# Group 0 of a decoder layer's attention: the softmax weights' low part ahead of the next maxima, the queries' low parts behind them

## The reference, cut to what matters

```python
q = (hidden_states @ Wq.T).reshape(b, s, H, D).transpose(0, 2, 1, 3)
scores = jnp.einsum('bhqd,bhkd->bhqk', q, k) * scale
scores = jnp.where(causal, scores, jnp.asarray(-1000000000.0, scores.dtype))
attn = jax.nn.softmax(scores, axis=-1)
out = jnp.einsum('bhqk,bhkd->bhqd', attn, v)
out = out.transpose(0, 2, 1, 3).reshape(b, s, H * D)
return out @ Wo.T
```

## Time and profile before

| | us |
|---|---|
| median of 3 executions | 1101.77 (1101.17 to 1103.44) |
| the profiled execution | 1102.57 |
| its span | 1100.8 |
| TensorE busy | 1061.0 (96% of the span) |
| VectorE busy | 905.5 (82%) |
| ScalarE busy | 530.6 (48%) |
| GpSimd busy | 410.9 (37%) |

### The profile page before, as it was taken

How to read it: one execution, slowest core, us unless ns; L and a number is a source line. 1 busy time by engine, 2 the same in 40 slices (tenths; PEclk the granted TensorE clock), 3 DMA queues, 4 the chain that set the end, 5 groups by cost and what they waited for, 6 DMA issues and landing times.

```text
span 1100.8 us, 19648 instructions
## 1 busy us (share of the span) xinstructions
PE 1061.0 (96%) x6229; PEld 565.9 (51%) x6236; DVE 905.5 (82%) x1861; ACT 530.6 (48%) x1081; POOL 410.9 (37%) x423
## 2 busy tenths in 40 slices
PE   6999988999999999999999999999999998969998
PEld 5976544555555555555555555555555554434443
DVE  7979588888797878788888888787978798889973
ACT  5665466545444545454545455454445454233420
POOL 2339654545343435344342434353434243000000
PEclk9999999999999999999999999999999999999999
DMA  8036156564454455454534554544445388224442
GB/s 318 11 106 240 39 113 145 139 140 96 126 136 114 98 138 137 107 131 114 136 101 118 133 120 110 134 124 114 107 118 138 81 194 235 103 42 89 100 97 86
DMA packets 229601, 135.74 MB, mean 123 GB/s; under 512 B 200112, under 2 KB 202288, under 8 KB 228656
## 3 DMA queue, kind: packets, MB, share of 16 engines
q1 hardware_dynamic: 229552, 135.11, 48.3%
HBM read 68.23 MB, written 17.83 MB: 78 GB/s over the span
## 4 chain that ended last, share of the span: by engine, by line
PE 85%; DVE 8%; ACT 3%; issue 2%; POOL 1%; DMA 1%; POOLq 0%; DVEq 0%; ACTq 0%; SPq 0%
PE ps L1710 82%; PE ps L1963 2%; ACT prob L1042 1%; DVE wo_sb L1196 1%; DVE prob L1435 1%; DVE h_b L1196 1%; PE ps L2034 1%; DMA wq_sb<-wo_in 1%; DVE prob_t L1196 1%; PE ps L1724 0%; DVE stats L1257 0%; DVE wq_sb L1196 0%; DVE o_t L1196 0%; DMA prob_t<-prob_s 0%; POOL prob L767 0%
## 5 line engine op out<-in xcount | busy, mean ns | idle before, releaser
L767 POOL TENSOR_SCALAR prob<-prob,row_inv 128x128 f32<-128x128 f32 (+3 forms) x256 | 203.3, 813 | 438.7 <-DVE row_inv L1406 438.7
L1710 PE MATMUL ps<-wo_sb,o_t 128*128 128x512 f16 x1536 | 351.3, 379 | 3.6 <-DVE x_sb L1417 3.6
L1710 PE MATMUL ps<-h_b,wq_sb 128*128 128x512 f16 x1524 | 345.6, 382 | 1.3 <-DVE wq_sb L1196 1.3
L1042 ACT ACTIVATE prob<-prob,neg_max 128x128 f32<-128x128 f32 (+3 forms) x256 | 140.6, 550 | 222.4 <-DVE neg_max L1441 222.4
L1710 PEld LDWEIGHTS ps<-h_b,wq_sb 128*128 128x128 f16 x1524 | 148.5, 98 | 179.9 <-issue 4.3
L1710 PEld LDWEIGHTS ps<-wo_sb,o_t 128*128 128x128 f16 x1536 | 147.3, 98 | 171.7 <-DVE x_sb L1417 6.3
L1417 DVE SCALAR_TENSOR_TENSOR x_sb<-ps,x_sb 128x512 f32<-128x512 f32 x256 | 174.0, 685 | 54.7 <-PE ps L1710 53.8
L1710 PE MATMUL ps<-prob_t,v_sb 128*128 128x128 f16 (+2 forms) x960 | 116.7, 275 | 7.2 <-DMA prob_t<-prob_s 7.2
L1710 PE MATMUL ps<-k_t,q_t 128*128 128x512 f16 (+3 forms) x768 | 114.8, 299 | 0.6 <-DVE neg_max L1441 0.6
L1435 DVE CUSTOM_DVE_ANT_0 prob<-ps,mask 128x512 f32<-128x512 f32 (+3 forms) x256 | 110.2, 483 | 2.3 <-issue 1.6
L1710 PEld LDWEIGHTS ps<-prob_t,v_sb 128*128 128x128 f16 x960 | 83.5, 98 | 37.6 <-DMA prob_t<-prob_s 8.0
(11 more groups left out here) (147 smaller groups left out, 1132.6 us busy)
## 6 DMA issues: line engine op xcount, KB each, us to landing
wq_in<-in_wq SPq DMA_DIRECT2D x64, 256.0 KB, 3.6
wo_in<-in_wo SPq DMA_DIRECT2D x32, 512.0 KB, 3.9
side_in<-in_ctx SPq DMA_DIRECT2D x16, 512.0 KB, 4.2
kv_parts<-wo_sb SPq DMA_DIRECT2D x7, 1024.0 KB, 5.4
x_sb<-in_x SPq DMA_DIRECT2D x8, 512.0 KB, 9.3
ctx_quantised<-side_out SPq DMA_DIRECT2D x16, 256.0 KB, 2.9
h_b<-ctx_quantised SPq DMA_DIRECT2D x2, 2048.0 KB, 11.0
out<-x_sb SPq DMA_DIRECT2D x8, 512.0 KB, 2.9
```

The costliest lines, as they stand in the source:

```text
L767: ins = nc.gpsimd.tensor_scalar(at, at, row_inv[:, u % 2, q:q + 1], S_P, ALU.mult, ALU.mult)
L1042: ins = nc.scalar.activation(at, at, ACT.Exp, bias=neg_max[:, n % 2, q:q + 1], scale=SOFTMAX, accum_out=row_sum[:, n % 2, q:q + 1])
L1710: ins = nc.tensor.matmul(out_, lhs(i), rhs(j), start=start and n == 0, stop=stop and n == 3 * len(pairs) - 1)
```

## The change

In group 0, from u = 1 on, VectorE takes p_split(g, u-1) ahead of maxima(g, u) instead of behind them. The low parts of the queries of step u-1, which stood at the end of step u-1, now come right behind maxima(g, u). The low parts of step 7's queries stay at the end of step 7. In all other groups the order is as it was. No other engine's list changes.

```diff
--- before.py
+++ after.py
@@ -1456,8 +1456,14 @@
                 for u in range(UNITS):
                     queries = not (last and u >= PAIR_UNITS)
                     s = u % PAIR_UNITS
+                    if first and u > 0:
+
+                        p_split(g, u - 1)
                     maxima(g, u)
-                    if not (first and u == 0):
+                    if first and u > 0:
+                        for unit in STEP_UNITS[(u - 1) % PAIR_UNITS]:
+                            q_part(g, u - 1, unit)
+                    if not first:
                         p_split(g, u - 1)
                     step_add(g, u, 0)
                     inverses(g, u)
@@ -1491,7 +1497,7 @@
                             combine(g, u, n)
                     step_add(g, u, 2)
                     step_add(g, u, 3)
-                    if queries:
+                    if queries and (not first or u == UNITS - 1):
                         for unit in STEP_UNITS[s]:
                             q_part(g, u, unit)
                     if s == 3 and not last:
```

## The result

The changed kernel takes 1114.01 us, the median of four executions (1112.41 to 1114.38), the kernel before beside it 1102.41 (1101.17 to 1103.44). The ratio is 1.0098, with a 95% interval of 1.0085 to 1.0110: slower by about 11 us. The forecast was 1112.3 us, with 1104.5 to 1116.0 as range, and a chance of 0.87 for slower.

What follows compares the result with a forecast made beforehand. TensorE, busy 85% of a 1100.8 us span, was taken as the bound, group 0's delay reaching the end. Adding 10.5 gave 1111.3, with 1.77 around it 1113.1, less 0.8 to the median 1112.3 us; range 1104.5 to 1116.

Steps and rivals of the forecast that it cites:

- H: Time when ScalarE's high part of the previous step's weights is ready; VectorE now stands at the step's head until then.
- C: End of VectorE's work of the previous step; neg_max(u) was to end at max(C, H) + 1.49 + 1.93.
- the carried shift: Delay of neg_max passed from step to step in group 0: +3.5 us in step 1, +11.1 in step 7.
- S(7): TensorE's scores of step 7 in group 0, forecast to start at 208.0 us instead of 198.73.
- The wait that I had set the sum on: TensorE's wo chunks of step 6 wait for VectorE's wo_sb low part, forecast to end at 196.6 us, not 185.96.
- SyncE: A Wq load of step 2 comes some 2.5 us later, its reader 5.85 us later: cost taken as zero.
- The clock: TensorE's clock drops after waits in group 0: taken as 0, though by the skill's rule 1.4 us more.
- Contention on p_lo: VectorE's low part of the weights slowed by GpSimd: taken as 0, bounded at 0 to 1.4 us each.
- Faster: Rival, chance 0.08: the transposes' 7.2 us and the clock's 1.4 go, giving 1093 us; decided at H = C.
- Half: Rival, chance 0.15: VectorE's work fits under GpSimd and the weights' high part, 10.45 us a step; 1104 to 1108 us.
- (a): Group 0's q_t low parts go behind the next maxima, under a 2.75 us wait; step 2's two took 3.07 us.
- (b): The previous step's low part of the weights goes ahead of the maxima, so VectorE stands until H in group 0.

Runs made afterwards that it cites:

- experiment 7: The changed kernel with a second PSUM bank for outputs(1) and outputs(3) of group 0: ratio 1.0083 to the kernel before, group 0 90.74 us.
- step 4 alone: The kernel before with VectorE's low part of the weights ahead of the maxima in step 4 of group 0 only: ratio 0.9998.
- experiment 6: The changed kernel, ScalarE taking the weights' high part before its q_t high parts, three of four group 0 normalising instructions left out: 1.0041; without leaving them out 1.0085.
- its control: The kernel before with the same ScalarE reordering and three of four normalising instructions left out in group 0: ratio 1.0010, group 0 81.1 us.
- experiment 2: The kernel before with only the q_t low parts moved behind the next maxima and the weights' low part in group 0: ratio 0.9961, 1099.95 against 1103.80 us.
- step 1 alone: The kernel before with VectorE's low part of the weights ahead of the maxima in step 1 of group 0 only: ratio 1.0024.
- the short normalising: Three of four GpSimd normalising instructions left out in group 0: ratio 0.9990 in the kernel before, 1.0085 in the changed kernel.

## Why the prediction was right

**The bound.** TensorE has no wait from 220 to 900 us in the changed kernel, so group 0's loss reached the end at full size. Right.

**The shifts, step by step.** The changed kernel's group 0 began 1.03 us late, which is taken off here. neg_max(1) to neg_max(7) end, by these rows, at 142.9, 153.3, 165.4, 178.8, 189.6, 201.6 and 214.0:

```profile
143.75 0.17 DVE L1441 TENSOR_SCALAR neg_max<-row_max 128x4 f32<-128x4 f32 x1
...
154.18 0.17 DVE L1441 TENSOR_SCALAR neg_max<-row_max 128x4 f32<-128x4 f32 x1
...
166.29 0.17 DVE L1441 TENSOR_SCALAR neg_max<-row_max 128x4 f32<-128x4 f32 x1
...
179.62 0.17 DVE L1441 TENSOR_SCALAR neg_max<-row_max 128x4 f32<-128x4 f32 x1
...
190.49 0.17 DVE L1441 TENSOR_SCALAR neg_max<-row_max 128x4 f32<-128x4 f32 x1
...
202.45 0.17 DVE L1441 TENSOR_SCALAR neg_max<-row_max 128x4 f32<-128x4 f32 x1
...
214.85 0.17 DVE L1441 TENSOR_SCALAR neg_max<-row_max 128x4 f32<-128x4 f32 x1
```

Forecast were 142.95, 153.45, 165.65, 179.55, 190.45, 202.5 and 214.7: each within 1 us. The largest new miss is step 4: I had kept the 2.38 us of the Wq block's low part, and it took 1.93, beside a GpSimd sum into ctx_sum that took 2.12 instead of 2.57. So H against C and the carried shift were the right model.

**TensorE.** S(7) was forecast at 208.0, and came at 208.11 - 1.03 = 207.1; group 1 at 220.3, and came at 219.5. Group 0 cost 9.7 where I had 10.5. The wait that I had set the sum on was there: the wo_sb low part ended at 196.83 - 1.03 = 195.8, forecast 196.6, and TensorE began 0.1 us behind it. The medians lie 11.6 us apart; the 1.9 beyond group 0's 9.7 come from no step of the forecast, they are the scatter named above.

**What was missing** is a kind of wait, the o_t bank (6.4 us). It did not spoil the sum because it is off the path (experiment 7), which was luck, since I had not weighed it, but it did spoil my expectation for step 4 alone, where it would have been the next to end. S(5) waited 1.08 us for a q_t part, which now lies behind maxima(4), and not for neg_max(4); I had called these readers late enough. S(2) and S(3) waited 0.52 and 0.23 us for neg_max, which I had not listed, and product 2 did not wait for copy_p1. And of the waits on transposes none stayed, where I had kept the first. Its second transpose was issued at the same time as before (142.22 - 1.03 = 141.19), but outputs(0), forecast at 146.09, came at 145.78 - 1.03 = 144.75. Why it landed earlier is open. It brought nothing, since the next query product waited 1.32 us for a combine.

**The terms taken at zero.** SyncE: right, no wait on a Wq load. The clock: right, granted 1.00 over the stretch, no drop, and so not the 1.4 us more that I had set beside the sum. That the drop of the kernel before went away needed no credit, since the sum goes by VectorE's times and picks TensorE up behind it, at the wo chunks. It does mean that the new order costs about 11 us, of which 1.3 come back as clock. Contention on p_lo: 1.49 us in six steps, 1.77 in step 7, where I had put an overlap of 0.7 us: 0.3 us lost. The q_t parts fell to 0.68 to 0.69 us in all seven cases up to step 7, as forecast.

**The rivals.** "Faster" was to be decided at H = C, and step 4 alone is that case: no loss, but no gain either. Nor does H decide alone: in experiment 6 p_hi is ready in time in nearly every step, and group 0 is still 3.7 us longer than its control. The gain that this rival saw behind the point H = C was wrong for want of the wait for the exponentials that p_lo had covered. "Half", the bare loop of 10.45 us a step, came in steps 2 and 5 alone (10.4 and 10.9 us from one neg_max to the next). In step 4 VectorE's own work does not fit under p_hi, and in steps 3, 6 and 7 p_hi stands behind the q_t high parts on ScalarE: 12.0 to 13.3 us.

**The reading that was too simple** came only with the experiments: I took the stall to be mostly GpSimd's, though my own sum for steps 3, 6 and 7 had ScalarE's q_t high part in it. And (a), the q_t parts, was the half that pays: 3.07 us of it stood in the prediction as a gain inside step 2, hidden by (b).

## What to carry to other kernels

Before an instruction is put at the head of an in-order queue, ask when its input is ready and what stands behind it: if the input comes from a loop that the queue itself feeds (here row_inv, GpSimd, ScalarE and back), the head of the queue is a bad place for it, and work with all its inputs ready (the maxima) belongs in front. An instruction with slack is best placed under a wait that is there in any case; moving it away lays that wait bare, and moving another one there (the q_t parts, 0.4% faster alone) was the gain here, a part of it through the clock. Test the halves of a compound reordering apart, and don't take a long entry in a list of waits for a cost until taking it away has moved the end. Before two traces are subtracted, compare the granted clock of their stretches: here a slow stretch in one of them was worth 1.3 us of a difference of 3.7.

## What the runs showed of the hardware

The clock drop does not follow the length of a wait. In the changed kernel TensorE waited 3.24 us before S(4), with the granted clock at 1.00 throughout; with p_lo alone ahead it waited 3.61 us there, and S(4) took 3.36 us instead of 1.79, at a granted clock of 0.50, the 1.2 GHz level; with step 1 alone it waited 2.46, and S(4) again took 3.36, at 0.52. In the kernel before, a wait of 2.94 us before outputs(2) had no drop behind it (1.00 from 163 to 168 us), and the shorter one of 2.28 us before outputs(3) had.

The low parts of q_t and of Wq blocks take 0.68 us while GpSimd is idle, and one of a Wq block took 0.68 beside its normalising too (at 151.04 in the kernel before). Beside GpSimd's sums two q_t parts took up to 3.17 us (step 4 alone, at 200.87) and one up to 2.59 (experiment 2, at 206.28). And a row of VectorE with one SBUF input was slowed as well: the rounding into side_out took 0.68 us in the kernel before at 151.64 and 1.75 in the changed kernel with the short normalising, where it ran into GpSimd's sums for Wq:

```profile
155.84 1.75 DVE L1561 TENSOR_SCALAR side_out<-side_in 128x1024 bf16<-128x1024 f32 x1
```
